# A scan and a gated MLP fused over blocks of tokens: the order of the work at each block's turn

## The chip, the core and the metric

The kernel runs on one core of a Trainium2 chip. The metric is the device time of one execution in microseconds, as the median of several runs. A core has five engines that work through programs of their own and meet at semaphores: TensorE (PE, matrix products), VectorE (DVE), ScalarE (ACT, functions by table), GpSimd (POOL) and SyncE (SP, which starts transfers here). Every engine takes its instructions strictly in the order of its program.

## What is computed

The program is a stack of eight layers on 4096 tokens of 256 numbers, each with a norm before and a norm behind it, and a residual sum. The change touches the fifth and the sixth, a state-space scan (attention's place in layer 2) and a gated MLP:

```python
x = x + _layernorm(_L2_attn_ref(_layernorm(x), ...))
x = x + _layernorm(_L2_ffn_ref(_layernorm(x), ...))

def _L2_attn_ref(x, ...):                     # 512 channels, 16 states
    xc, z = split(x @ in_proj)
    xs = silu(causal_conv4(xc) + conv_b)
    dt, Bm, Cm = split(xs @ x_proj)           # 64, 16, 16
    dt = softplus(dt @ dt_proj + dt_proj_b)
    h = exp(dt * A) * h + dt * Bm * xs        # a scan over time, for each channel and state
    y = sum_states(h * Cm) + D * xs
    return (y * silu(z)) @ out_proj

def _L2_ffn_ref(x, ...):                      # 1024 hidden
    h = silu(w1(x) * s) * (w2(x) * s)
    h = gelu(h1(h) * s)
    h = gelu(h2(h) * s)
    return w3(h) * s
```

## The kernel before

`scan_and_mlp` (line 2099) does both layers in one pass. The tokens are cut into NB = 8 blocks of 512. A loop of nine **steps** n = 0 to 8 runs in every engine: step n does the scan of block n, the scan layer's output product, norms and MLP of block b = n - 1, and the last product and norm of the MLP of block b2 = n - 2. What begins a step, between the last scan of one block and the first of the next, is called the **turn** below.

**Units.** The scan of a block is 64 units k = 0 to 63: 16 states by 4 groups of 128 channels, two groups in the first half (k below 32) and two in the second. Unit k is one exponential on ACT (`exponential`, line 2490, into one of two PSUM banks, so it may run at most two units ahead of the scans), one product on POOL (`unit_product`, 2293, into one of DR = 4 buffers), one scan on DVE (`scan`, 2648, needs both), one product with C on DVE (`times_c`, 2659) and one sum on POOL (`unit_sum`, 2300). The MLP's and the norms' instructions on ACT, DVE, POOL and SP are hung on unit numbers: `if k == 1: post.scalar(...)` puts the scale of a norm behind exponential 1.

**The step size.** Before the first unit, `dt` has to be made: the product `dt` on PE (2375), Abs, Exp and Ln on ACT (2518, 2523, 2527), `dt_linear`, `one_plus` and `step_size` on DVE (2620, 2626 to 2631, 2637 to 2639). Abs writes into `ea`, which is the array `ys` of the block before, so it waits until DVE has gated that block's output (`gated`, 2588 and 2591, counted by `y_ready`).

**PSUM.** All PE results outside the scan go through LB = 4 banks in the fixed order of the list `groups`: a product may start when the result four places before it has been read out (`bank_for`, `taken`). Gate and up of the MLP's first layer are groups of two matmuls each; the hidden layers' groups `hid` of eight; `out` is the MLP's last product, `y` the scan layer's output product, `z` and `in` the two input projections, `xp` the projection x_dbl, `turn` and `turn_l` transposes.

**The MLP on ACT.** `silu_gate` (SiLU on a gate, into one of two buffers) ran in units 9 to 16, one a unit, and DVE's `up_times_gate` (2665) in 8 to 15, one a unit. `GELUS` names the units behind which ACT does two GELUs each. The functions belong to different tables: where Exp and SiLU or GELU follow each other, a load of the table (ACT_TABLE_LOAD) stands between.

**The norms** are made in four parts: statistics on DVE (108, 111), the reciprocal root on POOL (1135 to 1140), the scale on ACT (1145), and for `post` the residual sum on POOL (2304). `post` is behind the scan layer, `pre_l` ahead of the MLP, `post_l` behind it, `pre` ahead of the next scan.

**Transfers.** SP loads the MLP's weights into a ring of WR = 4 buffers of 512 KB (`weights_to`), and the rows of B and C (`bc_load`); the loop of units sets the order of both.

## Time and profile before

| | us |
|---|---|
| median of 3 runs | 5377.04 |
| lowest and highest run | 5374.46 and 5400.65 |
| the profiled execution | 5403.7 |
| its span, first to last instruction | 5401.9 |
| instructions in it | 77,523 |
| PE, DVE, ACT, POOL busy | 4553.4, 3586.3, 2659.0, 2315.1 |

The trace gives every instruction of one execution with its start and its length, and for an engine that stood idle the instruction whose end released it. The fused stage runs from 1940 us to about 3880 us of the span. Step 3 lies in the trace from 2605 us to 2828 us, and stands for steps 2 to 6, whose DVE instructions follow the same pattern.

### The profile page before, as it was taken

How to read it: one execution, taken by the hardware profiler on the slowest of the kernel's cores; microseconds unless marked ns; L12 is line 12 of the kernel's file. 1: busy time of each engine (PE TensorE's matmuls, PEld its weight loads, DVE VectorE, ACT ScalarE, POOL GpSimd, SP SyncE). 2: the span in 40 equal slices, each digit the busy share in tenths (PEclk: the TensorE clock that was granted, in tenths of full speed). 3: DMA queues.
4: the chain of work that ended last, by engine and by line, in shares of the span. 5: the costliest groups of instructions: out<-in, count | busy, mean ns of one | idle time of the engine just before them, and what ended most of it. 6: DMA issues, size and time to landing. Idle time of an engine off the chain costs nothing. (4 is left out here: it accounts for less than half of the span.)

```text
span 5401.9 us, 77523 instructions
## 1 busy us (share of the span) xinstructions
PE 4553.4 (84%) x23572; PEld 2292.7 (42%) x23572; DVE 3586.3 (66%) x5800; ACT 2659.0 (49%) x4933; POOL 2315.1 (43%) x2615
## 2 busy tenths in 40 slices
PE   8799999777978821889888898898879999999598
PEld 4233333443447510344444444444434444444365
DVE  7788887466744468787787877883156666667521
ACT  3466667101323232655656556563137767767221
POOL 4122222323733548768677686784002222222311
PEclk9899999788987965889999899999989999999899
DMA  4111111013223433445354453452131111111000
GB/s 121 54 33 33 33 33 28 6 39 84 55 84 94 110 94 81 122 112 150 107 147 119 116 148 112 139 136 94 56 115 45 45 43 44 53 43 33 18 1 31
DMA packets 261917, 406.64 MB, mean 75 GB/s; under 512 B 53154, under 2 KB 140731, under 8 KB 261307
## 3 DMA queue, kind: packets, MB, share of 16 engines
q1 hardware_dynamic: 254687, 383.81, 25.1%
q0 software_dynamic: 6912, 18.88, 1.4%
q8 instruction: 164, 2.69, 0.2%
q14 instruction: 154, 1.26, 0.1%
HBM read 349.26 MB, written 52.54 MB: 74 GB/s over the span
## 5 line engine op out<-in xcount | busy, mean ns | idle before, releaser
L893 DVE CUSTOM_DVE_ANT_0 banks<-banks,l3s_table 128x1024 f32<-128x1024 f32 x512 | 629.1, 1229 | 307.6 <-PE banks L815 299.9
L999 ACT ACTIVATE l3s_probs<-banks,l3s_far_now 128x512 f32<-128x512 f32 (+4 forms) x1280 | 599.1, 513 | 299.0 <-PE banks L831 154.9
L2293 POOL TENSOR_TENSOR l_dbx<-l_u,l_bc 128x512 f32<-128x512 f32 x512 | 670.7, 1314 | 166.1 <-DVE l_u L2639 164.1
L888 DVE TENSOR_REDUCE l0s_peak<-banks 128x1 f32<-128x1024 f32 x512 | 609.5, 1212 | 141.5 <-PE banks L815 140.7
L2300 POOL TENSOR_TENSOR l_ys<-l_ys,l_hc 128x512 f32<-128x512 f32 x480 | 615.8, 1283 | 183.1 <-DVE l_hc L2659 180.4
L999 ACT ACTIVATE l0s_probs<-banks 128x512 f32<-128x512 f32 x1024 | 535.2, 601 | 275.6 <-PE banks L831 275.3
L2490 ACT ACTIVATE banks<-l_dt,l_decay 128x512 f32<-128x512 f32 x512 | 347.3, 688 | 444.8 <-DVE banks L2648 441.4
L2420 PE MATMUL banks<-l_hb,l_ring 128*128 128x512 f32 x1024 | 455.5, 608 | 19.9 <-issue 19.8
L2420 PE MATMUL banks<-l_ha,l_ring 128*128 128x512 f32 x1024 | 444.2, 594 | 20.2 <-ACT l_hb L2471 10.2
L2648 DVE TENSOR_TENSOR_SCAN banks<-banks,l_carry,l_dbx 128x512 f32<-128x512 f32 x256 | 329.6, 1289 | 137.2 <-ACT banks L2490 96.7
L2648 DVE TENSOR_TENSOR_SCAN banks<-banks,l_dbx 128x512 f32<-128x512 f32 x256 | 314.2, 1229 | 131.3 <-ACT banks L2490 75.1
L831 PE MATMUL banks<-l3s_q_st,l3s_k_st 98*128 98x512 bf16 x1024 | 363.2, 386 | 26.9 <-issue 16.7
L815 PE MATMUL banks<-l3s_k_st,l3s_q_st 96*128 96x512 bf16 x1024 | 318.6, 394 | 48.0 <-PEq L473 27.3
L815 PE MATMUL banks<-l0s_k_st,l0s_q_st 96*128 96x512 bf16 x1024 | 314.6, 389 | 46.5 <-PEq L473 27.0
L2659 DVE TENSOR_TENSOR l_hc<-banks,l_bc 128x512 f32<-128x512 f32 x480 | 325.6, 679 | 0.7 <-POOL l_ys L2300 0.7
L2420 PEld LDWEIGHTS banks<-l_hb,l_ring 128*128 128x128 f32 x1024 | 199.0, 195 | 276.0 <-issue 275.1
L831 PE MATMUL banks<-l0s_q_st,l0s_k_st 98*128 98x512 bf16 x1024 | 309.7, 381 | 5.8 <-ACT l0s_probs L999 2.0
L2420 PEld LDWEIGHTS banks<-l_ha,l_ring 128*128 128x128 f32 x1024 | 193.1, 190 | 267.5 <-issue 254.5
L837 PE MATMUL banks<-l3s_band_parts,identb 128*128 128x220 bf16 (+2 forms) x1920 | 297.2, 263 | 0.0
L848 PE MATMUL banks<-l0s_probs,l0s_vs 128*32 128x256 f32 x4096 | 273.5, 385 | 12.9 <-issue 10.2
L848 PE MATMUL banks<-l3s_probs,l3s_vs 128*32 128x256 f32 x4096 | 277.8, 389 | 1.2 <-ACT l3s_probs L999 0.9
L2407 PE MATMUL banks<-l_xtl,l_ring 128*128 128x512 f32 x512 | 242.0, 626 | 9.8 <-issue 5.7
(446 smaller groups left out, 7830.5 us busy)
## 6 DMA issues: line engine op xcount, KB each, us to landing
l_bc<-l_bc_rows SPq DMA_DIRECT2D x256, 512.0 KB, 5.4
l_ring<-in_l2f_stream SPq DMA_DIRECT2D x176, 512.0 KB, 7.1
l3s_table<-bias_tables SPq DMA_DIRECT2D x16, 960.0 KB, 4.4
y_rows<-l1f_out_b SPq DMA_DIRECT2D x80, 128.0 KB
qk_parts<-l0q_q_parts SPq DMA_DIRECT2D x48, 128.0 KB
qk_parts<-l0q_k_parts SPq DMA_DIRECT2D x48, 128.0 KB
l0s_q_st<-qk_parts SPq DMA_DIRECT2D x64, 96.0 KB
l0s_k_st<-qk_parts SPq DMA_DIRECT2D x64, 96.0 KB
```

The lines of the kernel that those rows point to most:

```text
L815: last = nc.tensor.matmul(s1[t % 2][:, half * 512:(half + 1) * 512], q_st[b % BATCH][0:STACK, t * P:(t + 1) * P], moving(k_st[b % BATCH], ...
L831: last = nc.tensor.matmul(scores, k_st[b % BATCH][0:STACK + 2, t * P:(t + 1) * P], moving(q_st[b % BATCH], STACK + 2, half), start=True, s ...
L848: last = nc.tensor.matmul(outT[q * 32:(q + 1) * 32, :], vs[b % 2][:, kt, :], probs[b % 2][:, kt, q * QUARTER:(q + 1) * QUARTER], start=(kt ...
L888: nc.vector.tensor_reduce(out=peak[:, b % 2, t:t + 1], in_=s1[t % 2], axis=AX, op=ALU.max, negate=True).then_inc(s1_used, 1)
L893: nc.vector.tensor_tensor_reduce(out=s1[t % 2], in0=s1[t % 2], in1=rows, scale=1.0, scalar=LOW, op0=ALU.add, op1=ALU.max, accum_out=peak[: ...
L999: last = nc.scalar.activation(columns(probs[b % 2][:, t, :], c0, c1), scores[:, c0 - half * 512:c1 - half * 512], ACT.Exp, scale=scale, **add)
L2293: nc.gpsimd.tensor_tensor(dbx[:, k % DR], u[:, mt], bc[:, load % BR, 0], ALU.mult).then_inc(dbx_ready, 1)
L2300: nc.gpsimd.tensor_tensor(ys[:, mt], ys[:, mt], hc[:, k % CR], ALU.add).then_inc(add_done, 1)
L2420: last = nc.tensor.matmul(banks[:, bank, :], w[:, c * P:(c + 1) * P], src[:, c, :], start=(c == 0), stop=(c == HT - 1))
L2490: nc.scalar.activation(banks[:, DA + m2, :], dt[:, mt], ACT.Exp, scale=decay[:, mt, st:st + 1])\
L2648: nc.vector.tensor_tensor_scan(out=banks[:, H + m2, :], data0=banks[:, DA + m2, :], data1=dbx[:, k % DR], initial=start, op0=ALU.mult, op1 ...
L2659: nc.vector.tensor_tensor(hc[:, k % CR] if st else ys[:, mt], banks[:, H + m2, :], bc[:, load % BR, 1], ALU.mult).then_inc(hc_ready, 1)
```

## The change

The order of the instructions, and nothing else, is changed. (1) At the turn PE does the output product `y` of the block that has just been scanned first, then the `dt` products, then the MLP's `out` of the block before it; ACT empties `y` ahead of its Abs instructions. (2) The statistics, roots, scales and the residual of `post`, and of `pre_l`, go from units 1 to 5 into the turn (on ACT the scale of `pre_l` goes to unit 1), and with them the SiLUs of z to unit 1 and the reading of `turn_l` to unit 5; the second half of `step_size` goes from unit 1 to unit 5. (3) `GATES` lets ACT do two SiLUs behind each of the units 9, 12, 15, 18, and DVE one `up_times_gate` in that unit and one in the next. (4) The GELUs, the reading of the next block's projections and its SiLUs go to later units.

```diff
--- before.py
+++ after.py
@@ -2112,3 +2112,4 @@
     ADDS = UNITS - CT
-    GELUS = {22: 0, 28: 2, 33: 4, 39: 6, 45: 8, 50: 10, 56: 12, 61: 14}
+    GELUS = {24: 0, 30: 2, 35: 4, 41: 6, 49: 8, 54: 10, 59: 12, 63: 14}
+    GATES = {9: 0, 12: 2, 15: 4, 18: 6}
     LOADS = UNITS // 2
@@ -2167,5 +2168,5 @@
             groups += [f"xp{n}"] if n < NB else []
-            groups += [f"out{b2}.0"] if b2 >= 0 else []
-            groups += [f"dt{n}.{i}" for i in range(CT) if n < NB]
             groups += [f"y{b}.{i}" for i in range(2) if b >= 0]
+            groups += [f"dt{n}.{i}" for i in range(CT) if n < NB]
+            groups += [f"out{b2}.0"] if b2 >= 0 else []
             groups += [f"z{n}.{i}" for i in range(CT) if n < NB]
@@ -2276,4 +2277,4 @@
                         weights_to(first + k // 2)
-                    if n and k in (11, 13, 15, 17):
-                        weights_to(first + 5 + (k - 11) // 2)
+                    if n and k in (11, 13, 16, 19):
+                        weights_to(first + 5 + (11, 13, 16, 19).index(k))
                     if n and k in GELUS:
@@ -2311,2 +2312,6 @@
                 b, b2 = n - 1, n - 2
+                if b >= 0:
+                    post.gpsimd(g, b)
+                    residual(b)
+                    pre_l.gpsimd(g, b)
                 for k in range(UNITS):
@@ -2316,8 +2321,2 @@
                             unit_sum(n, k - DR)
-                    if k == 1 and b >= 0:
-                        post.gpsimd(g, b)
-                    if k == 3 and b >= 0:
-                        residual(b)
-                    if k == 5 and b >= 0:
-                        pre_l.gpsimd(g, b)
                     if k == 8 and b2 >= 0:
@@ -2432,7 +2431,2 @@
                     project_dbl(n)
-                if b2 >= 0:
-                    mlp_out(b2, 0)
-                if n < NB:
-                    for i in range(CT):
-                        project_dt(n, i)
                 if b >= 0:
@@ -2442,2 +2436,7 @@
                     for i in range(CT):
+                        project_dt(n, i)
+                if b2 >= 0:
+                    mlp_out(b2, 0)
+                if n < NB:
+                    for i in range(CT):
                         project_z(n, i)
@@ -2513,2 +2512,5 @@
                 b, b2, more = n - 1, n - 2, n + 1 < NB
+                if b >= 0:
+                    for i in range(2):
+                        take(f"y{b}.{i}", rows[:, 2 * i:2 * i + 2, :].rearrange("p k d -> p (k d)"))
                 if n < NB:
@@ -2519,2 +2521,5 @@
                             .then_inc(abs_done, 1)
+                if b >= 0:
+                    post.scalar(act, b, lambda t: rows[:, t, :], lambda t: rows[:, t, :]).then_inc(post_ready, 1)
+                if n < NB:
                     for i in range(2):
@@ -2527,5 +2532,2 @@
                         nc.scalar.activation(dt[:, half], eb[:, half], ACT.Ln).then_inc(ln_ready, 1)
-                if b >= 0:
-                    for i in range(2):
-                        take(f"y{b}.{i}", rows[:, 2 * i:2 * i + 2, :].rearrange("p k d -> p (k d)"))
                 for k in range(UNITS):
@@ -2534,4 +2536,5 @@
                     if k == 1 and b >= 0:
-                        post.scalar(act, b, lambda t: rows[:, t, :], lambda t: rows[:, t, :]).then_inc(post_ready, 1)
-                    if k == 3 and n < NB:
+                        pre_l.scalar(act, b, lambda t: tokens(b)[:, t, :], lambda t: rows_l[:, t, :])\
+                            .then_inc(rows_l_ready, 1)
+                    if k == 1 and n < NB:
                         wait(act, y_ready, 2 * n)
@@ -2540,5 +2543,2 @@
                     if k == 5 and b >= 0:
-                        pre_l.scalar(act, b, lambda t: tokens(b)[:, t, :], lambda t: rows_l[:, t, :])\
-                            .then_inc(rows_l_ready, 1)
-                    if k == 7 and b >= 0:
                         for c in range(KC):
@@ -2548,4 +2548,5 @@
                             .then_inc(post_l_ready, 1)
-                    if 9 <= k < 9 + HT and b >= 0:
-                        silu_gate(b, k - 9)
+                    if k in GATES and b >= 0:
+                        silu_gate(b, GATES[k])
+                        silu_gate(b, GATES[k] + 1)
                     if k == 21 and more:
@@ -2557,9 +2558,9 @@
                         gelu(b, GELUS[k] + 1)
-                    if k == 33 and more:
+                    if k == 36 and more:
                         for c in range(KC):
                             take_turned(n + 1, c)
-                    if k in (40, 42) and more:
-                        take_x(n + 1, k - 40)
-                        take_x(n + 1, k - 39)
-                    if k == 58 and more:
+                    if k in (43, 44) and more:
+                        take_x(n + 1, 2 * (k - 43))
+                        take_x(n + 1, 2 * (k - 43) + 1)
+                    if k == 59 and more:
                         for i in range(CT):
@@ -2674,4 +2675,5 @@
                     gated(b, 1)
-                if b2 >= 0:
-                    scale_out(b2, 0)
+                    for i in range(2):
+                        moved(v, f"y{b}.{i}")
+                    post.statistics(v, lambda k: rows[:, k, :])
                 if n < NB:
@@ -2680,8 +2682,10 @@
                     one_plus(n, 0)
+                if b >= 0:
+                    v.wait_ge(added, n)
+                    pre_l.statistics(v, lambda t: tokens(b)[:, t, :])
+                if n < NB:
                     one_plus(n, 1)
                     step_size(n, 0)
-                if b >= 0:
-                    for i in range(2):
-                        moved(v, f"y{b}.{i}")
-                    post.statistics(v, lambda k: rows[:, k, :])
+                if b2 >= 0:
+                    scale_out(b2, 0)
                 if n < NB:
@@ -2694,7 +2698,4 @@
                         times_c(n, k)
-                    if k == 1 and n < NB:
+                    if k == 5 and n < NB:
                         step_size(n, 1)
-                    if k == 3 and b >= 0:
-                        v.wait_ge(added, n)
-                        pre_l.statistics(v, lambda t: tokens(b)[:, t, :])
                     if k == 6 and b2 >= 0:
@@ -2703,4 +2704,5 @@
                         post_l.statistics(v, lambda t: scaled[:, t, :])
-                    if 8 <= k < 8 + HT and b >= 0:
-                        up_times_gate(b, k - 8)
+                    for j in (0, 1):
+                        if k - j in GATES and b >= 0:
+                            up_times_gate(b, GATES[k - j] + j)
                     if k == 18 and more:
```

ACT_TABLE_LOAD stands 280 times in ACT's program before, and 217 times now. The three places below are those on which the times rest. Names are those of the arrays; `l` in front stands for the stage.

On ACT, step 2's turn, from the reading of x_dbl to the SiLUs of z, before (`l_ys` takes Abs and Exp, `l_dt` Ln, `l_rows` the reading of `y` and the scale of `post`):

```order
L2471 ACTIVATE l_x_dbl<-banks 96x512
L2518 ACTIVATE l_ys<-banks,l_dt_b 128x512 x4
L2523 ACTIVATE l_ys<-l_ys 128x1024 x2
L2527 ACT_TABLE_LOAD
L2527 ACTIVATE l_dt<-l_hc 128x1024 x2
L2471 ACTIVATE l_rows<-banks 128x512 x2
L2490 ACT_TABLE_LOAD
L2490 ACTIVATE banks<-l_dt,l_decay 128x512 x2
L1145 ACTIVATE l_rows<-l_rows,l_post_shift,l_post_rstd 128x256 x4
L2490 ACTIVATE banks<-l_dt,l_decay 128x512 x2
L2471 ACT_TABLE_LOAD
L2471 ACTIVATE l_zs<-banks 128x512 x4
```

and now:

```order
L2470 ACTIVATE l_ha<-banks,l_sc 128x512 x2
L2470 ACTIVATE l_x_dbl<-banks 96x512
L2470 ACTIVATE l_rows<-banks 128x512 x2
L2520 ACTIVATE l_ys<-banks,l_dt_b 128x512 x4
L1145 ACTIVATE l_rows<-l_rows,l_post_shift,l_post_rstd 128x256 x4
L2528 ACT_TABLE_LOAD
L2528 ACTIVATE l_ys<-l_ys 128x1024 x2
L2532 ACT_TABLE_LOAD
L2532 ACTIVATE l_dt<-l_hc 128x1024 x2
L2489 ACT_TABLE_LOAD
L2489 ACTIVATE banks<-l_dt,l_decay 128x512 x2
L1145 ACTIVATE l_hb<-x,l_pre_l_shift,l_pre_l_rstd 128x256 x4
```

The reading of `y` and the scale of `post` now stand ahead of the Exp, the last two GELUs behind the last exponential, and a table load ahead of the Exp on `l_ys`.

On PE, the same turn, before:

```order
L2368 MATMUL banks<-l_xs,l_w_x 96x512 x4
L2396 MATMUL banks<-l_ring,l_ha 128x256 x16
L2375 MATMUL banks<-l_x_dbl,l_w_dt 128x512 x4
L2384 MATMUL banks<-l_w_out,l_xs 128x256 x16
L2360 MATMUL banks<-l_xt,l_w_in 128x512 x8
L2396 MATMUL banks<-l_ring,l_ha 128x256 x16
L2341 MATMUL banks<-ident,l_hb 128x128 x8
```

and now:

```order
L2367 MATMUL banks<-l_xs,l_w_x 96x512 x4
L2383 MATMUL banks<-l_w_out,l_xs 128x256 x16
L2374 MATMUL banks<-l_x_dbl,l_w_dt 128x512 x4
L2395 MATMUL banks<-l_ring,l_ha 128x256 x16
L2359 MATMUL banks<-l_xt,l_w_in 128x512 x8
L2395 MATMUL banks<-l_ring,l_ha 128x256 x16
L2340 MATMUL banks<-ident,l_hb 128x128 x8
```

`y` (array `l_w_out`) stands behind the projection x_dbl (array `l_w_x`) at once; `dt` and `out` (array `l_ring` with `l_ha`) stand behind it.

On DVE, the same turn from behind the end of gating, before (`l_hb<-banks,l_so` is the scaling of `out`):

```order
L2614 TENSOR_TENSOR l_hb<-banks,l_so 128x256 x2
L2620 TENSOR_SCALAR l_u<-banks,l_dt_b 128x512 x4
L2626 TENSOR_SCALAR l_hc<-l_ys 128x1024
L2628 SCALAR_TENSOR_TENSOR l_ys<-l_hc,l_ys 128x1024
L2631 TENSOR_TENSOR l_ys<-l_u,l_ys 128x1024
L2626 TENSOR_SCALAR l_hc<-l_ys 128x1024
L2628 SCALAR_TENSOR_TENSOR l_ys<-l_hc,l_ys 128x1024
L2631 TENSOR_TENSOR l_ys<-l_u,l_ys 128x1024
L2637 TENSOR_TENSOR l_dt<-l_dt,l_ys 128x1024
L2639 TENSOR_TENSOR l_u<-l_dt,l_xs 128x1024
L108 BN_STATS l_post_stats<-l_rows 128x6 x4
L111 BN_AGGR l_post_mean_var<-l_post_stats 128x2 x4
```

and now:

```order
L2621 TENSOR_SCALAR l_u<-banks,l_dt_b 128x512 x4
L2627 TENSOR_SCALAR l_hc<-l_ys 128x1024
L2629 SCALAR_TENSOR_TENSOR l_ys<-l_hc,l_ys 128x1024
L2632 TENSOR_TENSOR l_ys<-l_u,l_ys 128x1024
L108 BN_STATS l_pre_l_stats<-x 128x6 x4
L111 BN_AGGR l_pre_l_mean_var<-l_pre_l_stats 128x2 x4
L2627 TENSOR_SCALAR l_hc<-l_ys 128x1024
L2629 SCALAR_TENSOR_TENSOR l_ys<-l_hc,l_ys 128x1024
L2632 TENSOR_TENSOR l_ys<-l_u,l_ys 128x1024
L2638 TENSOR_TENSOR l_dt<-l_dt,l_ys 128x1024
L2640 TENSOR_TENSOR l_u<-l_dt,l_xs 128x1024
L2615 TENSOR_TENSOR l_hb<-banks,l_so 128x256 x2
```

The statistics of `post` (the same two rows, right behind gating and ahead of this piece now) and those of `pre_l` stand ahead of and inside the chain that makes the step size, and the scaling of `out` behind it.

## Rows read from the trace of the kernel before

**Rows 1.** Windows: busy us of PE, PEld, DVE, ACT, POOL; PE clock; DMA share; GB/s

```profile
2626.00:2850.00 224.00, 197.24 (x480) 95.34 (x480) 180.86 (x210) 133.00 (x171) 167.97 (x144) 0.93 0.46 127
```

**Rows 2.** Timeline of DVE at step 3's turn: start, length, engine, line, operands, idle before

```profile
2604.81 1.23 DVE L2591 TENSOR_TENSOR l_xs<-l_xs,l_zs 128x1024 f32<-128x1024 f32 x1
...
2611.38 1.23 DVE L2628 SCALAR_TENSOR_TENSOR l_ys<-l_hc,l_ys 128x1024 f32<-128x1024 f32 x1
...
2618.53 1.23 DVE L2639 TENSOR_TENSOR l_u<-l_dt,l_xs 128x1024 f32<-128x1024 f32 x1
2619.67 1.40 DVE L108 BATCH_NORM_STATS2 l_post_stats<-l_rows 128x6 f32<-128x256 f32 x4
...
2621.45 2.43 DVE L2648 TENSOR_TENSOR_SCAN banks<-banks,l_carry,l_dbx 128x512 f32<-128x512 f32 x2
```

**Rows 3.** Timeline of PE at the same turn

```profile
2598.77 2.84 PE L2375 MATMUL banks<-l_x_dbl,l_w_dt 64*128 64x512 f32 x6
...
2608.82 8.41 PE L2384 MATMUL banks<-l_w_out,l_xs 128*128 128x256 f32 x32
```

**Rows 4.** Timeline of ACT and of POOL at the same turn

```profile
2609.51 1.99 ACT L2523 ACTIVATE l_ys<-l_ys 128x1024 f32<-128x1024 f32 x2
...
2624.26 2.07 ACT L1145 ACTIVATE l_rows<-l_rows,l_post_shift,l_post_rstd 128x256 f32<-128x256 f32 x4 [3.78 <-POOL l_post_shift L1140]
...
2622.29 0.20 POOL L1135 TENSOR_TENSOR l_post_rstd<-l_post_mean_var,eps 128x4 f32<-128x4 f32 x1
...
2624.03 0.20 POOL L1140 TENSOR_TENSOR l_post_shift<-l_post_shift,l_post_rstd 128x4 f32<-128x4 f32 x1
```

**Rows 5.** Timeline of PE and of ACT where step 8 begins, after an idle PE

```profile
3697.61 10.13 PE L2384 MATMUL banks<-l_w_out,l_xs 128*128 128x256 f32 x32 [7.92 <-DVE l_xs L2591]
...
3704.32 0.60 ACT L2471 ACTIVATE l_rows<-banks 128x512 f32<-128x512 f32 x1 [18.20 <-PE banks L2384]
```

**Rows 6.** Timeline of DVE: scans of units 10, 20, 37, 38, 46, 57, 63

```profile
2656.09 1.28 DVE L2648 TENSOR_TENSOR_SCAN banks<-banks,l_carry,l_dbx 128x512 f32<-128x512 f32 x1
...
2665.54 0.75 DVE L2665 SCALAR_TENSOR_TENSOR l_ha<-banks,l_sc,l_hb 128x512 f32<-128x512 f32 x1
2667.55 1.29 DVE L2648 TENSOR_TENSOR_SCAN banks<-banks,l_carry,l_dbx 128x512 f32<-128x512 f32 x1 [1.25 <-ACT banks L2490]
...
2691.13 1.26 DVE L2648 TENSOR_TENSOR_SCAN banks<-banks,l_carry,l_dbx 128x512 f32<-128x512 f32 x1
...
2733.32 1.29 DVE L2648 TENSOR_TENSOR_SCAN banks<-banks,l_carry,l_dbx 128x512 f32<-128x512 f32 x1
...
2743.45 1.28 DVE L2648 TENSOR_TENSOR_SCAN banks<-banks,l_carry,l_dbx 128x512 f32<-128x512 f32 x1
...
2765.85 1.29 DVE L2648 TENSOR_TENSOR_SCAN banks<-banks,l_carry,l_dbx 128x512 f32<-128x512 f32 x1 [6.48 <-ACT banks L2490]
...
2808.76 1.29 DVE L2648 TENSOR_TENSOR_SCAN banks<-banks,l_carry,l_dbx 128x512 f32<-128x512 f32 x1
...
2821.47 1.29 DVE L2648 TENSOR_TENSOR_SCAN banks<-banks,l_carry,l_dbx 128x512 f32<-128x512 f32 x1
```

**Rows 7.** Timeline of ACT and PE in the gates' units, of POOL behind them

```profile
2663.53 1.28 ACT L2471 ACT_TABLE_LOAD   x1
...
2665.61 3.67 PE L2407 MATMUL banks<-l_xtl,l_ring 128*128 128x512 f32 x8 [0.34 <-issue]
...
2706.56 14.00 PE L2420 MATMUL banks<-l_ha,l_ring 128*128 128x512 f32 x32 [1.24 <-DMA l_ring<-in_l2f_stream]
...
2707.88 1.26 POOL L2293 TENSOR_TENSOR l_dbx<-l_u,l_bc 128x512 f32<-128x512 f32 x1
...
2710.34 1.27 POOL L2293 TENSOR_TENSOR l_dbx<-l_u,l_bc 128x512 f32<-128x512 f32 x1
```

**Rows 8.** Timeline of ACT at unit 45's GELUs and at unit 58

```profile
2763.12 0.69 ACT L2471 ACTIVATE l_ha<-banks,l_sc 128x512 f32<-128x512 f32 x1 [5.57 <-PE banks L2420]
...
2805.77 1.67 ACT L2484 ACTIVATE l_xs<-l_xs 128x512 f32<-128x512 f32 x3
```

8 lines of the change are left out of this document (4 added, 4 removed).

## The prediction

> **What bounds the kernel now.** I read in this order: the busy time by stretch, the timelines of all engines across one turn, then the scans of one block on DVE, each with what ended the idle time before it. In a full step no engine is busy all the time: of 224 us PE works 197, DVE 181, POOL 168, ACT 133 [rows 1]. So the length of a step is not the work of one engine but a chain that changes hands, and the reader should follow the scans, since every block needs all 64 of them and they are on the chain at each place. Step 3 is taken for steps 2 to 6. The gating of the old block begins at 2604.81 and the first new scan at 2621.45, 16.6 us of turn [rows 2]. The later scans give the stretches of the block [rows 2, 6]: unit 0 to 10 takes 34.6 us, 10 to 20 35.0, 20 to 37 42.2, 37 to 38 (the other gating) 10.1, 38 to 46 22.4, 46 to 57 (the four convolutions) 42.9, 57 to 63 12.7. Undisturbed, DVE needs 2.0 us for a unit's scan and product (2665.54 to 2667.55 is one gate product and a wait of 1.25 us that ACT ended, so a gate unit takes 4.0) [rows 6]. POOL needs 2.46 us for a unit (2707.88 to 2710.34) [rows 7]. From 10 to 20 ACT bounds, from 20 to 37 POOL; at unit 46 DVE waits 6.48 us, because ACT sits in front of a GELU for 5.57 us, which PE had not reached [rows 6, 8].
>
> **The turn.** The zero of the times in this part is 2606.0, the end of gating (2604.81 + 1.23), and the first scan stands at 15.4 [rows 2]. Three of the four `dt` products were then already done, at 2598.77, in the shadow of the last scans [rows 3]. That is what the new order takes away: `y` needs the gated block, so it can't start before 0, and everything behind it on PE, `dt` too, waits for it. The cost of `y` is 8.41 us if PE comes from work [rows 3] and 10.13 behind an idle stretch of 7.92, with the first half only there 6.7 us after the start [rows 5]. PE will have been idle for over 10 us here (it has nothing left but x_dbl), so I take 10.1 and keep 8.4 for the range. Then:
> - four `dt` at 0.95 (2.84 / 3) to 13.9, the last Abs (0.7) to 14.6 (Abs as a GELU) [rows 3, 8];
> - beside it ACT reads `y` (0.60, to 10.8), DVE does the statistics (1.40, and 0.4 for the four small ones behind, from 2619.67 to 2621.45) to 12.6, POOL the roots (2622.29 to 2624.23, 1.9) to 14.5 [rows 2, 4, 5];
> - ACT scales `post` (2.07) to 16.7, loads the table for Exp (1.28, new here: the last thing on ACT is now a GELU) to 18.0, first Exp (1.0) to 19.0 [rows 4, 7];
> - DVE: `one_plus` (0.7 + 1.25 + 1.25 = 3.2, its middle instruction) to 22.2 [rows 2], statistics of `pre_l` (1.8) to 24.0 (the residual is there by then), second `one_plus` 3.2 to 27.2, `step_size` (2 x 1.25) to 29.7;
> - POOL's first product (1.26) to 31.0; with the scaling of `out` and hand-overs the first scan is at 31.4 instead of 15.4 [rows 2, 7].
>
> The turn gets **16 us longer**.
>
> **Unit 0 to 10, 4.7 us shorter.** Ten units at 2.0, the half `step_size` of 2.5 (4.5 before, when POOL's residual ran beside it, so 2.5 to 4.5), `out`'s scaling and statistics 2.5, together 25. Waits: the scale of `pre_l`, the SiLUs of z and two loads (2.1 + 2.4 + 2.6) hold exponential 2 back so that DVE waits 3.3; reading `turn_l` costs 0.9, since `out`'s second half, which waits for z's banks, puts the transposes at about unit 5; the root of `post_l` on POOL holds its product 9 back, 1.5. With 0.8 less for the first scan pair: 29.9.
>
> **Unit 10 to 20, 2.4 us shorter.** Loads fall from 16 to 8 a step here, so ACT would need only 3 x 0.69 + 2 x 0.69 + 2 x 1.28 = 6.0 us for three units [rows 7, 8]. But the four banks now bind: up j + 2 may be computed when DVE has read up j, and gate j + 3 stands behind it. One cycle of three units is: scan 1.29, product 0.67, `up_times_gate` 0.75, two PE groups 3.67, SiLU 0.69, load 1.28, exponential 0.69 = 9.1 us, against 7.4 for POOL's three units and 12.0 for three before [rows 6, 7, 8]. The gates stretched over twelve units instead of eight, so the gain is small: 9.6 for 10 to 13 (POOL adds the residual `residual_l` of 2.3 here, which the slow gate units hid before), 18.4, and 4.6 for the last unit with the statistics of `pre`: 32.6.
>
> **Unit 20 to 57.** POOL keeps its pace of 2.46, so 20 to 37 stays 42.2; PE gets to the hidden layers some 20 us later than before: the first needs the last gate product, which stands 31.4 + 29.9 + 32.6 + 2.8 = 97 us behind gating instead of 15.4 + 34.6 + 6.5 x 4.0 = 76, and two GELUs wait for it, 0.8 in all. 38 to 46 loses its wait: the GELUs are at unit 49 now, and PE, still some 16 us late, is through before; 22.4 becomes 16.7, **5.7 less**. 46 to 57 is DVE's own work and stays.
>
> **Unit 57 to 63, 3.8 us longer.** The block's SiLUs used to start on ACT at 2805.77, in the shadow of the last convolution (DVE's next scan is at 2808.76) [rows 6, 8]. Now they follow two GELUs behind exponential 59: 1.28 + 1.37 + 1.28 + 2.5 + 1.28 + 0.69 = 8.4 us until the next exponential, of which DVE has 3.9 in hand; it waits 4.5. The wait of 0.8 at unit 61's GELUs goes.
>
> **SP and the rest.** The weights' loads go later with the GELUs, each still behind the product that frees its buffer, at least 7 us ahead of its user; one such wait is 1.24 now [rows 7], taken as unchanged. Loads of B and C don't move.
>
> **Sum.** A full step: 16.0 - 4.7 - 2.4 + 0.8 - 5.7 + 3.8 = +7.8, five times = 39. Step 1 has no `out` and no `post_l`, its table load is not new, and its gains in the gates are larger: +3. Step 7 has no next block, so neither the gain of 5.7 nor the loss of 3.8: +9. Step 0: +1. In step 8 `y` leads anyway and its `out` fills idle PE time: 0. Together +52: the profiled execution would go from 5403.7 to 5456. It lies 26.7 above the median of 5377.04, so I carry the difference over: **5429**.
>
> **A rule of the skill.** A table load takes 1.28 us in the trace, and the exponential follows at once (2663.53 + 1.28) [rows 7]. The program has 280 loads, 63 more than now; taken whole that is 81 us. The Trainium skill ("ScalarE: Activation LUTs", Table sets: the hidden batching unit) says to batch calls by set, which is what the pairs of gates do, and gives about 2.66 us for a switch with its drain; by that figure it would be 168 us, an estimate, and the sum would be a gain. The trace doesn't bear out the drain, and has ACT busy 133 of 224 us, so the rule counts only where ACT bounds.
>
> **Rivals.**
> 1. *The loads' whole time comes back.* If ACT set the pace of the whole step, 63 x 1.28 = 81 us and the six waits of about 6.2 us (37) come off, against seven turns (112) and six late SiLUs (23): +17; and as the late SiLUs wait for loads that the 81 has counted already, -6: 5371. For it speaks 12 us a step of ACT-bound gate units, against it POOL's 2.46 right behind them. If the turn were shorter too (`y` at 8.4, `post`'s scale and the load beside `dt`: 5 us), it would reach 5371 - 35 = 5336, the one way to a clearly faster kernel.
> 2. *The gates run at POOL's pace.* If PE's two groups are ready before ACT asks, 10 to 20 is 24.6 + 2.3 + 1.9 = 28.8, 3.8 less a step; PE is then early enough for the GELUs as well (0.8): 7.8 - 4.6 = 3.2, in all about +22: 5399, not slower by what can be told. It decides at a cycle of 8 us or less.
> 3. *PE becomes late.* The hidden layers start 20 us later, and two GELUs wait already. If the clock after the longer idle stretch makes y and z slower by 5 us, these waits grow one for one: +4 to 5 a step, +30: 5459 and more.
>
> **How the numbers follow.** Forecast (5405 to 5450) 0.55; rival 3 (5450 to 5485) 0.15; rival 2 and milder mixes (5385 to 5405) 0.13; rival 1 at 5371 0.10, at 5336 0.07. A measurement tells about 0.5% (27 us) from no change. Slower by more: 0.70 (0.55 + 0.15); within: 0.23 (0.13 + 0.10); faster: 0.07. The range goes from 5372 to 5475.
>
> **What would show it.** In the profile after: PE idle for over 10 us before L2383's first product, and that product ahead of dt; the first scan 31 us behind the end of gating; gate units with 9 us for three; no wait of 6 us for the GELUs in the convolutions' units; one wait of 4 to 5 us behind exponential 59. It would be wrong if the exponentials of `dt` didn't wait for `post`'s scale, or if steps came out at 224 us or less.

## The result and the profile after

| | before | after |
|---|---|---|
| median, measured side by side | 5386.72 us | 5468.94 us |
| lowest and highest run | 5374.46 and 5400.65 | 5456.45 and 5481.87 |
| the profiled execution, its span | 5403.7, 5401.9 | 5481.87, 5480.1 |
| ACT busy | 2659.0 | 2580.8 |

The changed kernel takes 1.0152 times as long (95% interval 1.0108 to 1.0196): 82 us more, where 52 were forecast. The time lies inside the range of 5372 to 5475, and the sign is the one forecast. But it lies 40 us above the forecast of 5429 and outside the band around it (5405 to 5450), in the band that rival 3 had been given with a chance of 0.15. 10 of these us are the kernel before, whose median is 5386.72 here where the forecast started from 5377.04; the other 30 have no term in the sum.

The change did what it says on ACT, 78 us less work there. None of it shows in the time. The chain of a step, read off the starts of DVE's scans as in [rows 2, 6], shows why. Each number is the mean of steps 2 to 6; the third column is what the prediction added.

| stretch | before | after | measured | predicted |
|---|---|---|---|---|
| turn (scan 63 to the next scan 0) | 23.0 | 39.0 | +16.0 | +16.0 |
| unit 0 to 10 | 34.6 | 29.7 | -4.9 | -4.7 |
| unit 10 to 20 | 35.0 | 34.9 | -0.1 | -2.4 |
| unit 20 to 38 | 52.3 | 52.4 | +0.1 | +0.8 |
| unit 38 to 46 | 23.1 | 16.7 | -6.4 | -5.7 |
| unit 46 to 57 | 42.9 | 46.6 | +3.7 | 0 |
| unit 57 to 63 | 12.7 | 16.2 | +3.5 | +3.8 |
| a step | 223.7 | 235.4 | +11.7 | +7.8 |

Five full steps cost 58.6 us more, step 1 14.9 (218.0 to 233.0), step 7 12.7 (195.0 to 207.7), step 0 0.3: 86.5 for steps 0 to 7. Everything else took 8.3 less in this execution, 7.0 of it ahead of the first scan (1982.8 to 1975.8), in layers that the change doesn't touch, so the span grew by 78.2.

**The turn.** The timeline of PE at step 3's turn, after (start, length, engine, line, operands, idle before; answers to [rows 3]):

```profile
2625.41 10.14 PE L2383 MATMUL banks<-l_w_out,l_xs 128*128 128x256 f32 x32 [5.97 <-DVE l_xs L2592]
2635.47 3.70 PE L2374 MATMUL banks<-l_x_dbl,l_w_dt 64*128 64x512 f32 x8
2639.10 7.17 PE L2395 MATMUL banks<-l_ring,l_ha 128*128 128x256 f32 x32
```

ACT in the same turn (answers to [rows 4]), and DVE (answers to [rows 2]):

```profile
2632.13 0.60 ACT L2470 ACTIVATE l_rows<-banks 128x512 f32<-128x512 f32 x1 [12.06 <-PE banks L2383]
...
2640.19 2.07 ACT L1145 ACTIVATE l_rows<-l_rows,l_post_shift,l_post_rstd 128x256 f32<-128x256 f32 x4 [0.29 <-POOL l_post_shift L1140]
2642.28 1.28 ACT L2528 ACT_TABLE_LOAD   x1
2643.57 2.01 ACT L2528 ACTIVATE l_ys<-l_ys 128x1024 f32<-128x1024 f32 x2
```

```profile
2624.13 1.23 DVE L2592 TENSOR_TENSOR l_xs<-l_xs,l_zs 128x1024 f32<-128x1024 f32 x1
2636.28 1.41 DVE L108 BATCH_NORM_STATS2 l_post_stats<-l_rows 128x6 f32<-128x256 f32 x4 [10.93 <-ACT l_rows L2470]
...
2644.66 0.69 DVE L2627 TENSOR_SCALAR l_hc<-l_ys 128x1024 f32<-128x1024 f32 x1 [3.64 <-ACT l_ys L2528]
...
2657.05 2.49 DVE L2649 TENSOR_TENSOR_SCAN banks<-banks,l_carry,l_dbx 128x512 f32<-128x512 f32 x2 [0.82 <-POOL l_dbx L2294]
```

The four `dt` products, of which three used to be done 4.4 us before gating ended, now end 13.8 us behind its end (2625.36). Exp waits for `post`'s scale and a table load, and the first scan stands 31.7 us behind gating. PE had been idle for only 5.97 us when `y` began, where the prediction expected over 10: it was late with the hidden layers and the projection x_dbl.

**The gates.** Windows of the three rounds of gates in step 3: us, busy us of PE, PEld, DVE, ACT, POOL (instructions), granted clock of PE, DMA share, GB/s.

```profile
2678.00:2687.50 9.50, 9.40 (x16) 3.84 (x16) 6.20 (x13) 4.94 (x7) 7.21 (x9) 0.76 0.43 150
2689.30:2698.20 8.90, 8.83 (x16) 3.53 (x16) 4.94 (x6) 5.86 (x8) 8.90 (x7) 0.81 0.82 174
2700.10:2707.30 7.20, 7.13 (x16) 2.96 (x16) 4.84 (x6) 4.80 (x6) 7.20 (x7) 1.00 0.35 76
```

The same 16 matmuls take 9.40, 8.83 and 7.13 us. A granted clock of 1.00 is the 2.4 GHz level; 0.76 and 0.81 mean that part of the stretch ran at 1.2 GHz. PE had stood idle for 6.79 us before the first round, 1.91 before the second and 1.97 before the third. Before the change it had pauses of 0.3 to 0.4 us in these units, and the clock stood at 1.00. Which rounds are slow differs from step to step: in steps 2 and 4 it is the first and the third, and a fourth round, of 12 matmuls, takes 7.1 us at 0.76 in steps 1 to 4, for what takes 5.4 at 1.00 (units_only below).

**The convolution.** DVE and POOL at the first convolution of step 3, after:

```profile
2793.92 0.67 DVE L2660 TENSOR_TENSOR l_hc<-banks,l_bc 128x512 f32<-128x512 f32 x1
2794.51 6.26 DVE L2599 TENSOR_SCALAR l_xs<-l_xc,l_taps,l_conv_b 128x512 f32<-128x512 f32 x1
2800.85 2.40 DVE L2602 SCALAR_TENSOR_TENSOR l_xs<-l_xc,l_taps,l_xs 128x512 f32<-128x512 f32 x3
```

```profile
2794.31 1.30 POOL L2294 TENSOR_TENSOR l_dbx<-l_u,l_bc 128x512 f32<-128x512 f32 x1
...
2799.20 1.30 POOL L2294 TENSOR_TENSOR l_dbx<-l_u,l_bc 128x512 f32<-128x512 f32 x1
2805.12 1.27 POOL L2301 TENSOR_TENSOR l_ys<-l_ys,l_hc 128x512 f32<-128x512 f32 x1 [4.63 <-DVE l_hc L2660]
```

The same instruction before took 0.93 us, and the three behind it 4.09:

```profile
2769.64 0.93 DVE L2598 TENSOR_SCALAR l_xs<-l_xc,l_taps,l_conv_b 128x512 f32<-128x512 f32 x1
2770.65 4.09 DVE L2601 SCALAR_TENSOR_TENSOR l_xs<-l_xc,l_taps,l_xs 128x512 f32<-128x512 f32 x3
```

POOL works through five instructions 1.22 us apart until 2800.5, and DVE's ends at 2800.8. Over the program this line grew from 43.6 to 75.8 us, 32.2 = 6 x 5.4: once a step, in steps 1 to 6. Step 0 had the long one before the change too (46 to 57 took 47.1 there).

**The last units.** DVE behind exponential 59, and PE's waits for weights:

```profile
2847.55 1.29 DVE L2649 TENSOR_TENSOR_SCAN banks<-banks,l_carry,l_dbx 128x512 f32<-128x512 f32 x1 [4.31 <-ACT banks L2489]
```

```profile
2813.23 14.00 PE L2419 MATMUL banks<-l_hb,l_ring 128*128 128x512 f32 x32 [1.65 <-DMA l_ring<-in_l2f_stream]
2835.29 16.15 PE L2419 MATMUL banks<-l_hb,l_ring 128*128 128x512 f32 x32 [8.06 <-DMA l_ring<-in_l2f_stream]
```

The first is the wait of 4.5 us that was forecast. The others are not: over the program PE waits 57.0 us for weights in the second hidden layer, where before it waited for none; the 8.0 us that it waited for them in the first hidden layer before are gone (the row of the page; busy us, mean ns | idle before, what ended it):

```profile
L2419 PE MATMUL banks<-l_hb,l_ring 128*128 128x512 f32 x1024 | 456.5, 607 | 57.2 <-DMA l_ring<-in_l2f_stream 57.0
```

### The profile page after: what moved, and what is told of

Its sections match the earlier page's. It is cut to its first block and busy times, and to the rows that moved or that the text cites. A ratio compares the mean times of both kernels' runs of the same rounds, so it can differ in the third digit from the quotient of the medians.

```text
span 5480.1 us, 77460 instructions
## 1 busy us (share of the span) xinstructions
PE 4565.1 (83%) x23572; PEld 2298.9 (42%) x23572; DVE 3583.6 (65%) x5800; ACT 2580.8 (47%) x4870; POOL 2327.1 (42%) x2615
## 5 line engine op out<-in xcount | busy, mean ns | idle before, releaser
L2294 POOL TENSOR_TENSOR l_dbx<-l_u,l_bc 128x512 f32<-128x512 f32 x512 | 658.5, 1291 | 69.3 <-DVE l_u L2640 57.2
L2406 PE MATMUL banks<-l_xtl,l_ring 128*128 128x512 f32 x512 | 272.0, 691 | 94.5 <-DVE l_ha L2666 41.1
L848 PE MATMUL banks<-l0s_probs,l0s_vs 128*32 128x256 f32 x4096 | 273.5, 385 | 12.8 <-issue 10.2
```

The source lines that it names most:

```text
L848: last = nc.tensor.matmul(outT[q * 32:(q + 1) * 32, :], vs[b % 2][:, kt, :], probs[b % 2][:, kt, q * QUARTER:(q + 1) * QUARTER], start=(kt ...
L2294: nc.gpsimd.tensor_tensor(dbx[:, k % DR], u[:, mt], bc[:, load % BR, 0], ALU.mult).then_inc(dbx_ready, 1)
```

## The experiments

Every kernel was timed beside the kernel before, whose median was between 5386 and 5398 us in these groups; ratios are to that. The table gives the same stretches for all (means of steps 2 to 6).

| kernel | ratio, 95% interval | turn | 0-10 | 10-20 | 20-38 | 38-46 | 46-57 | 57-63 | step |
|---|---|---|---|---|---|---|---|---|---|
| before | 1 | 23.0 | 34.6 | 35.0 | 52.3 | 23.1 | 42.9 | 12.7 | 223.7 |
| after | 1.0152 (1.0108, 1.0196) | 39.0 | 29.7 | 34.9 | 52.4 | 16.7 | 46.6 | 16.2 | 235.4 |
| turn_only | 1.0103 (1.0065, 1.0141) | 38.0 | 28.7 | 35.0 | 52.3 | 22.4 | 42.9 | 12.7 | 232.0 |
| units_only | 1.0028 (1.0010, 1.0046) | 26.2 | 34.6 | 34.5 | 52.4 | 16.7 | 46.6 | 16.2 | 227.2 |
| gates_only | 1.0033 (1.0011, 1.0054) | 23.0 | 34.6 | 35.0 | 55.3 | 21.0 | 42.9 | 12.7 | 224.4 |
| gelus_only | 1.0033 (1.0013, 1.0054) | 26.6 | 34.6 | 35.0 | 52.4 | 16.7 | 46.5 | 16.2 | 228.0 |
| y_first_norms_old | 1.0152 (1.0120, 1.0184) | 35.8 | 34.0 | 34.6 | 52.4 | 16.7 | 46.6 | 16.2 | 236.2 |
| gelus_last_back | 1.0155 (1.0128, 1.0183) | 37.6 | 29.1 | 34.0 | 52.4 | 16.7 | 46.6 | 19.1 | 235.5 |
| bank_early | 1.0103 (1.0074, 1.0131) | 38.4 | 28.4 | 35.2 | 52.4 | 16.7 | 46.6 | 16.2 | 233.9 |
| conv_stt | 1.0156 (1.0124, 1.0187) | 38.4 | 29.4 | 34.9 | 52.4 | 16.7 | 47.6 | 16.2 | 235.5 |
| last_back_loads_old | 1.0080 (1.0049, 1.0110) | 38.4 | 29.5 | 34.9 | 52.4 | 16.7 | 44.9 | 12.7 | 229.3 |
| gelu49_loads_old | 0.9942 (0.9918, 0.9966) | 23.0 | 34.6 | 35.0 | 52.3 | 16.0 | 44.1 | 12.7 | 217.8 |
| gelu49_pool_wait | 0.9915 (0.9892, 0.9939) | 23.0 | 34.6 | 35.0 | 52.3 | 16.0 | 42.6 | 12.7 | 216.2 |
| gelu49_pool_waits4 | 0.9866 (0.9843, 0.9889) | 24.1 | 34.6 | 35.0 | 52.3 | 16.0 | 38.5 | 12.7 | 213.2 |

### The change in parts

**turn_only**: the kernel after, with gates, GELUs and the loads and projections that go with them as before; only the turn is changed, items (1) and (2).

```diff
-    GELUS = {24: 0, 30: 2, 35: 4, 41: 6, 49: 8, 54: 10, 59: 12, 63: 14}
-    GATES = {9: 0, 12: 2, 15: 4, 18: 6}
+    GELUS = {22: 0, 28: 2, 33: 4, 39: 6, 45: 8, 50: 10, 56: 12, 61: 14}
...
-                    if k in GATES and b >= 0:
-                        silu_gate(b, GATES[k])
-                        silu_gate(b, GATES[k] + 1)
+                    if 9 <= k < 9 + HT and b >= 0:
+                        silu_gate(b, k - 9)
...
```

> The kernel before with the turn's new order alone: y first, both norms' steps moved up, the second step_size and the SiLUs of z moved; gates one a unit and GELUs, projections and SiLUs at the old units. Theory (the turn is the loss): the turn goes from 22.8 to 39 us in each of steps 2 to 6, units 0 to 10 from 34.6 to about 30, units 10 to 20 stay at 35 or more, the wait for the GELUs before unit 46 stays (22 to 24 us for units 38 to 46), so a step is 11 to 14 us longer and the kernel 75 to 100 us slower than before. Rival (the later units are the loss): the PE and ACT work keeps its old places, the gain at units 0 to 10 pays most of the turn, under 30 us slower.

Measured: ratio 1.0103, some 55 us, less than the 75 to 100 of my theory and more than the 30 of the rival. The turn alone grows by 15.0 us a step and units 0 to 10 give 5.9 back. So the turn is the largest part, 8.3 of the 11.7 us a step.

**units_only**: the kernel before with the new places of gates and GELUs and the old turn, items (3) and (4).

```diff
-    GELUS = {22: 0, 28: 2, 33: 4, 39: 6, 45: 8, 50: 10, 56: 12, 61: 14}
+    GELUS = {24: 0, 30: 2, 35: 4, 41: 6, 49: 8, 54: 10, 59: 12, 63: 14}
+    GATES = {9: 0, 12: 2, 15: 4, 18: 6}
...
```

> The kernel before with the later units alone: gates two at a time, GELUs, projections and SiLUs later; the turn as before. Theory (the turn is the loss): turn 22.8 and units 0 to 10 at 34.6 as before; units 10 to 20 between 30 and 35, units 38 to 46 down from 22.4 to 16.7, units 46 to 57 up from 42.9 to 46.6 (a slow first convolution), units 57 to 63 up from 12.7 to 16.2 (the block's SiLUs behind two GELUs), in all 0 to 5 us less a step, the kernel 0 to 35 us faster. Rival (the later units are the loss): 50 us slower or more.

Measured: 1.0028, a little slower where a gain was expected. 46 to 57 and 57 to 63 took what was expected; the turn didn't, it became 3.2 us longer though nothing in it had been moved.

The steps of this kernel also price the clock in the gates. Their instructions are the same, but the granted clock is not, and units 10 to 20 follow it. Windows of the last three rounds, in step 2 and in step 5 (us, busy us of PE (instructions), granted clock, DMA share, GB/s):

```profile
2442.59:2449.73 7.14, 7.13 (x16) 1.00 0.83 184
2452.26:2459.40 7.14, 7.13 (x16) 1.00 0.28 90
2461.37:2466.80 5.43, 5.43 (x13) 1.00 0.61 187
```

```profile
3122.08:3130.92 8.84, 8.83 (x16) 0.81 0.77 182
3132.89:3141.73 8.84, 8.83 (x16) 0.81 0.21 59
3143.69:3150.81 7.12, 7.12 (x13) 0.76 0.63 194
```

With all three at 1.00 the stretch takes 32.1 us (the prediction had 32.6), with one slow 33.8 (step 3), with two 34.9 (steps 4 and 6), with three 36.7.

**gates_only** and **gelus_only** split units_only once more: the line `GATES` with its users alone, and the line `GELUS` with the reading of projections and the SiLUs alone.

> The kernel before with the gates two at a time alone (SiLUs behind units 9, 12, 15, 18, products in the unit and the next, the weights' loads with them). Theory (the four banks bind the pairs): a cycle of three units takes 9 us at full clock, up to 11 us where the clock granted to PE is lower, so units 10 to 20 take 30 to 36 us against 35.0, and as PE starts the hidden layers later, the wait of 6 us for the GELUs at unit 46 grows and GELUs at units 22, 28 and 33 wait as well: 5 to 15 us more a step, the kernel 30 to 90 us slower. Rival (the table loads are the cost): 56 loads of 1.28 us come off the gates, units 10 to 20 fall to 29, the kernel 20 to 40 us faster.

Measured: 1.0033, 18 us where at least 30 were expected. In steps 2 to 6 units 10 to 20 stay at 35.0, although 8 table loads a step are gone; 20 to 38 is 3.0 longer, since PE then reaches the hidden layers later and ACT waits in front of early GELUs (3.73 us at 2703.19 in step 3). 38 to 46, which was expected to grow, is 2.1 shorter. The gates in pairs buy nothing on the chain.

> The kernel before with the later units for GELUs, projections and the block's SiLUs alone. Theory: units 38 to 46 fall from 22.4 to 16.7; the first convolution's first instruction takes about 6 us instead of 0.9, since POOL is then at work, so units 46 to 57 rise from 42.9 to 46.6; units 57 to 63 rise from 12.7 to about 16; in all 0 to +1 us a step, the kernel within 10 us of before. Rival (the convolution's length has another cause than POOL's work beside it): units 46 to 57 stay at 42.9 and the kernel is 20 us faster.

Measured: 1.0033, and 4.3 us a step where at most 1 was expected. The wait ahead of unit 46 is gone (-6.4), and 3.6, 3.5 and 3.6 come back in 46 to 57, in 57 to 63 and in the turn. The turn is seen on PE, just ahead of step 3 of gelus_only:

```profile
2575.84 3.60 PE L2368 MATMUL banks<-l_xs,l_w_x 128*96 128x512 f32 x8
2579.28 7.07 PE L2396 MATMUL banks<-l_ring,l_ha 128*128 128x256 f32 x32
2586.28 3.70 PE L2375 MATMUL banks<-l_x_dbl,l_w_dt 64*128 64x512 f32 x8
```

`out` (L2396) can't begin before the last GELU, which now stands at unit 63, and in the old order the `dt` products are behind it on PE: they start at 2586.28, behind the end of gating (2585.82), where three of them used to be done ahead of it [rows 3]. On ACT a table load is put ahead of Exp as well. In the kernel after `dt` is behind `y` anyway, and the turn grows by 16.0 us, not by 15.0 + 3.2: the two delays share 2.2. Over a whole step turn_only and units_only still add up (8.3 + 3.5 = 11.8 against 11.7), since the kernel after gives less back in the units than those two together (1.0 of it in units 0 to 10). It is gates_only and gelus_only that together cost more than units_only (0.7 + 4.3 against 3.5): the early GELUs for which gates_only waits stand later in units_only.

### Which half of the turn

**y_first_norms_old**: the kernel after, norms back in units 1 to 5, on DVE, ACT and POOL.

```diff
-                if b >= 0:
-                    post.gpsimd(g, b)
-                    residual(b)
-                    pre_l.gpsimd(g, b)
                 for k in range(UNITS):
...
+                    if k == 1 and b >= 0:
+                        post.gpsimd(g, b)
+                    if k == 3 and b >= 0:
+                        residual(b)
+                    if k == 5 and b >= 0:
+                        pre_l.gpsimd(g, b)
```

> The kernel after, with y's product still ahead of dt and out on PE, but with the norms' steps back where they were (scaling of post at unit 1, residual at 3, statistics and scaling of pre_l at 3 and 5, SiLUs of z at 3). It asks which half of the turn's edit lengthens it. My theory is that y's product ahead of dt is the larger part. From rows of the kernel with the turn's edit alone (end of gating 2598.70, y's product 9.18 us, first scan 2629.34, so 30.6 against 15.4 before): without post's scaling on ACT (2.07) and the statistics of pre_l between the two halves (1.8) and the 1.4 and 0.4 of post's statistics ahead of dt_linear, about 5 us of the 15.2 go, so the turn should be 33 to 35 us from the last scan of a block to the first of the next (39.0 in the kernel after, 22.8 before), while units 0 to 10 go back from 29.7 to 34.6. Per step nothing is gained: between 2 us shorter and 3 longer, the whole within 20 us of the kernel after, 5450 to 5490. The rival says that the norms' steps are what lengthens the turn, since PE has the whole time of the norms to catch up: then the turn is 27 us or less and the whole under 5430.

Measured: turn 35.8, units 0 to 10 34.0, ratio 1.0152 as the kernel after. So what is left of the change costs 12.8 of the turn's 16.0 us. 3.2 of it units_only has as well, from the late GELUs and their table load; `y` ahead of `dt` adds the other 9.6. The norms' steps only move between the turn and the units: 3.2 us on one side, 4.3 on the other. The rival (27 us) is out.

### The bank of `out` and the gates

**bank_early**

```diff
-                    if k == 6 and b2 >= 0:
+                    if k == 4 and b2 >= 0:
                         scale_out(b2, 1)
+                    if k == 6 and b2 >= 0:
                         v.drain()
```

> The kernel after, with one move: DVE scales the second half of out at unit 4 instead of unit 6 (its statistics stay at 6), which frees a bank that PE needs for the second gate. In the kernel after PE waits 6.79 us for that instruction and starts again at 2678.03, though out had been done at 2668.1. Unit 4 is worked at 2671, so PE starts 5 to 6 us earlier, and the second SiLU of a gate, which came at 2684.04 behind a wait of 4.52 us, is ready when ACT asks. My theory (the missing 2.4 us of units 10 to 20 and more went into this wait) gives 4.5 us less from unit 10 to 20: 30.4 instead of 34.9 in steps 2 to 6, nothing in step 1, in all 20 to 27 us less than the kernel after. The rival says that the gates' own round of PE, ACT and DVE at 10.8 us for three units sets the pace from the first pair on, so that an earlier start only moves a wait: then 10 to 20 stays above 33.5 and the whole within 8 us of the kernel after.

Measured: 10 to 20 at 35.2, so my theory falls for this stretch. The first pair of SiLUs does come without a wait, but then PE stands idle until `up_times_gate` frees a bank, and the next round is slow again:

```profile
2692.57 8.72 PE L2406 MATMUL banks<-l_xtl,l_ring 128*128 128x512 f32 x16 [5.36 <-DVE l_ha L2666]
```

The wait only moved. Against the kernel after the ratio is lower (1.0103 to 1.0152, with intervals that overlap), and steps 1 to 7 take 10 us less in the profiled executions, so something is gained, but in units 0 to 10 (1.3 a step) and the turn (0.6), not where I had looked for it. The turn's share is the clock over `y` again: `y` takes 8.67 us at 0.82 in step 3 and 10.02 at 0.71 in step 4, and the turn 37.6 and 39.0. With the windows above that leaves the rounds' own length. In the kernel after it is 10.8 us from one round's second SiLU to the next (2684.04 to 2694.84) where the 16 matmuls between take 8.83, and 9.1 (to 2703.95) where they take 7.13.

### The convolution

**conv_stt**

```diff
-                nc.vector.tensor_scalar(mine, xc[:, c, 0:TB], taps[:, c, 0:1], conv_b[:, c:c + 1], ALU.mult, ALU.add)
+                nc.vector.scalar_tensor_tensor(out=mine, in0=xc[:, c, 0:TB], scalar=taps[:, c, 0:1],
+                                               in1=conv_b[:, c:c + 1].to_broadcast([P, TB]), op0=ALU.mult, op1=ALU.add)
```

> The kernel after, with the first of the four steps of each convolution written as another instruction of DVE: a SCALAR_TENSOR_TENSOR that adds the bias as a broadcast operand, in place of the TENSOR_SCALAR; the values are the same. In the kernel after the first TENSOR_SCALAR (2794.51) takes 6.26 us against 0.93 before, and ends as POOL, which had run without a gap, falls idle; the SCALAR_TENSOR_TENSORs take 0.8 to 1.4 beside a busy POOL. My theory is that this form alone is held up while POOL has work without a gap. Then the stretch of units 46 to 57 falls from 46.6 to 42 to 44, 3 to 4 us a step in seven steps, and the whole is 18 to 28 us under the kernel after. The rival says that any large instruction of DVE would be held there, since what matters is that POOL has four units in hand: then the new first step takes 5 us or more too, the stretch stays at 46 or above and the time doesn't change.

Measured: the other instruction takes 6.51 us in the same place, and the stretch is 47.6. The form is not the cause; the rival holds.

```profile
2797.75 6.51 DVE L2599 SCALAR_TENSOR_TENSOR l_xs<-l_xc,l_taps,l_conv_b 128x512 f32<-128x512 f32 x1
2804.34 2.40 DVE L2603 SCALAR_TENSOR_TENSOR l_xs<-l_xc,l_taps,l_xs 128x512 f32<-128x512 f32 x3
```

### The last GELUs, and the loads behind them

**gelus_last_back**

```diff
-    GELUS = {24: 0, 30: 2, 35: 4, 41: 6, 49: 8, 54: 10, 59: 12, 63: 14}
+    GELUS = {24: 0, 30: 2, 35: 4, 41: 6, 49: 8, 54: 10, 56: 12, 61: 14}
...
-                    if k == 59 and more:
+                    if k == 58 and more:
```

> The kernel after, with only its last two pairs of GELUs back at units 56 and 61 and the block's SiLUs back at 58. My theory is that the SiLUs behind two GELUs and the exponential of unit 59 cost the 4.31 us that DVE waits at 2847.55, and that GELUs at unit 63 leave the table of GELU on ACT, so that the exponential of dt pays a load (1.28 at 2642.28) in the turn. So the stretch of units 57 to 63 falls from 16.1 to 12.7 and the turn from 39.0 to 37.7: 4.7 us a step, 33 us for six to seven steps, and the whole comes to 5427 to 5445. The rival says that with an earlier GELU PE, which runs late behind the longer turn, isn't there yet, and DVE waits at units 56 and 61 instead: then 46 to 57 grows by what 57 to 63 loses, and the whole stays within 10 us of the kernel after.

Measured: 1.0155, no gain. The turn did get 1.4 us shorter and the wait behind exponential 59 went, but 57 to 63 took 19.1. ACT, then DVE, at unit 61:

```profile
2871.56 0.69 ACT L2470 ACTIVATE l_ha<-banks,l_sc 128x512 f32<-128x512 f32 x1 [6.18 <-PE banks L2419]
```

```profile
2874.28 1.29 DVE L2649 TENSOR_TENSOR_SCAN banks<-banks,l_carry,l_dbx 128x512 f32<-128x512 f32 x1 [7.51 <-ACT banks L2489]
```

PE was late, and not from the longer turn. It had waited 8.29 us for weights:

```profile
2855.02 16.50 PE L2419 MATMUL banks<-l_hb,l_ring 128*128 128x512 f32 x32 [8.29 <-DMA l_ring<-in_l2f_stream]
```

SP issues the loads at the units of `GELUS`, so a later unit number also moved the loads; this pair was issued at unit 54 (2847.62).

**last_back_loads_old**: the same with a table of their own for SP's loads.

```diff
+    LOADS_AT = {22: 0, 28: 2, 33: 4, 39: 6, 45: 8, 50: 10, 56: 12, 61: 14}
...
-                    if n and k in GELUS:
-                        weights_to(first + 10 + GELUS[k])
+                    if n and k in LOADS_AT:
+                        weights_to(first + 10 + LOADS_AT[k])
```

> The kernel after, with its last two pairs of GELUs back at units 56 and 61 and the block's SiLUs at 58 (as in gelus_last_back, which gained nothing), and now also with SP's loads of the hidden layers' weights back at the units of the kernel before (22, 28, 33, 39, 45, 50, 56, 61). In gelus_last_back units 57 to 63 took 19.3 us, since PE had waited 8.29 us for weights (2855.02) whose load SP had issued at unit 54 (2847.62). My theory, formed from that run, is that the loads' place, and not the length of the turn, makes PE late at unit 61. Then PE has no such wait, units 57 to 63 take 12.7 to 13.5, the turn stays at 37.6, and the whole is 35 to 45 us under gelus_last_back, 5440 to 5452 beside 5398 of the kernel before. The rival says that PE is late from the longer turn itself (its hidden layers start 20 us later): then it still isn't there at unit 61, 57 to 63 stays at 17 or more, and the gain is under 15 us.

Measured: 1.0080, 57 to 63 at 12.7. The 88 us that gelus_last_back stood over its own before became 43. The gain of 45 us is the upper end of what was expected, because 46 to 57 fell too (46.6 to 44.9), which I had not foreseen.

### Is there a faster kernel

**gelu49_loads_old**: the kernel before, with the one move that had gained and nothing that had cost.

```diff
-    GELUS = {22: 0, 28: 2, 33: 4, 39: 6, 45: 8, 50: 10, 56: 12, 61: 14}
+    GELUS = {22: 0, 28: 2, 33: 4, 39: 6, 49: 8, 52: 10, 56: 12, 61: 14}
+    LOADS_AT = {22: 0, 28: 2, 33: 4, 39: 6, 45: 8, 50: 10, 56: 12, 61: 14}
...
-                    if n and k in GELUS:
-                        weights_to(first + 10 + GELUS[k])
+                    if n and k in LOADS_AT:
+                        weights_to(first + 10 + LOADS_AT[k])
```

> The kernel before, with the GELUs of unit 45 moved to 49 and those of 50 to 52, the last two pairs, the SiLUs and all loads where they are. My theory: units 38 to 46 lose the wait of 6.5 us (22.4 to 23.7 down to 16.7), and about 3.7 us of it come back in units 46 to 57, since POOL, no longer held up behind DVE's wait, works without a gap when the first convolution starts, whose first instruction then takes 6 us instead of 0.93; the last stretch and the turn stay (12.7 and 22.8). So 2 to 3 us a step in six steps, 12 to 18 us, ratio 0.997. The rival says that the slow convolution belongs to the later hidden layers and not to POOL: then 46 to 57 stays at 42.9 and the whole is 35 us faster, ratio 0.993.

Measured: 0.9942, between theory and rival. 38 to 46 lost 7.1, and only 1.2 of it came back. The instruction of 6 us that the theory expected isn't there. The wait ahead of unit 46 is gone and POOL works without a gap, as in the kernel after, yet the first convolution of step 3 begins like this, on DVE and on POOL:

```profile
2741.43 1.01 DVE L2599 TENSOR_SCALAR l_xs<-l_xc,l_taps,l_conv_b 128x512 f32<-128x512 f32 x1
2742.51 4.94 DVE L2602 SCALAR_TENSOR_TENSOR l_xs<-l_xc,l_taps,l_xs 128x512 f32<-128x512 f32 x3
```

```profile
2740.88 1.28 POOL L2301 TENSOR_TENSOR l_ys<-l_ys,l_hc 128x512 f32<-128x512 f32 x1
2742.10 1.46 POOL L2294 TENSOR_TENSOR l_dbx<-l_u,l_bc 128x512 f32<-128x512 f32 x1
```

DVE waits for the one POOL instruction that is under way, and then the two take turns. The convolution costs about 1 us more than before, and not 3.6.

**gelu49_pool_wait**

```diff
                         unit_product(n, k)
+                        if k == 49 and n + 1 < NB:
+                            wait(g, conv_ready, (n + 1) * CT + 1)
```

> gelu49_loads_old with one wait more: behind its product for unit 49 POOL waits until the first convolution of the next block is done, so that it is idle while DVE works on it. My theory is that DVE's first instruction there is held up by POOL's unbroken work. Then it takes 0.7 to 1.4 us instead of 6.3, units 46 to 57 take 41.5 to 43.5 instead of 46.6 in all seven steps that have convolutions (step 0 too, 47.1 so far), POOL's later products come in time but for a wait of DVE of about 1 us, and the whole is 32 to 40 us under the kernel before, ratio 0.993. The rival says that POOL's work has to be done anyway, and that DVE pays at the next units what it saved (POOL needs 2.46 us for a unit, DVE 2.0): then the stretch stays above 45.5 and the ratio at 0.997.

Measured: 0.9915, the stretch at 42.6 in every step, in step 0 too (47.1 before). The long first instruction, which this family still had in step 0, fell from 6.88 to 2.02 us there. In step 3 the whole first convolution went from 6.03 to 4.36 us. POOL's work, held back by a few microseconds, didn't come back as a wait of DVE; 0.3 us came back as longer second and third convolutions. The median against that of gelu49_loads_old, in the same group, is 12.0 us lower; the two intervals overlap, the steps' stretches do not.

**gelu49_pool_waits4**

```diff
-                        if k == 49 and n + 1 < NB:
-                            wait(g, conv_ready, (n + 1) * CT + 1)
+                        if k in (49, 52, 55, 58) and n + 1 < NB:
+                            wait(g, conv_ready, (n + 1) * CT + (k - 46) // 3)
```

> gelu49_pool_wait, with POOL held in the same way for the other three convolutions: behind its products for units 52, 55 and 58 it waits until convolution 2, 3 and 4 of the next block is done. In gelu49_pool_wait the second convolution's three SCALAR_TENSOR_TENSORs take 4.10 us with two POOL instructions beside them (1.44 and 1.72), where the same three took 2.40 with POOL idle. My theory: each convolution lasts as long as POOL's work beside it, so an idle POOL takes up to 1.7 us off each of the last three and up to 2.5 off the first; but POOL starts each stretch 1 to 2 us later, and DVE then waits for its products for part of it. So units 46 to 57 go from 42.6 to 39 to 41 us in seven steps, 11 to 25 us under gelu49_pool_wait, ratio 0.988 to the kernel before. The rival says that POOL's 2.46 us for a unit against DVE's 2.0 between two convolutions leaves nothing to hold back: what DVE saves in a convolution it waits for POOL right behind it, the stretch stays at 42 or above, and the ratio at 0.991.

Measured: 5324.59 us, 0.9866 (0.9843 to 0.9889), the fastest kernel here: 1.3% under before, 2.8% under the kernel after. The fourth convolution of step 3 on DVE, and POOL beside it:

```profile
2755.11 0.84 DVE L2601 TENSOR_SCALAR l_xs<-l_xc,l_taps,l_conv_b 128x512 f32<-128x512 f32 x1
2756.02 3.25 DVE L2604 SCALAR_TENSOR_TENSOR l_xs<-l_xc,l_taps,l_xs 128x512 f32<-128x512 f32 x3
```

```profile
2755.60 1.48 POOL L2294 TENSOR_TENSOR l_dbx<-l_u,l_bc 128x512 f32<-128x512 f32 x1
2759.36 1.27 POOL L2301 TENSOR_TENSOR l_ys<-l_ys,l_hc 128x512 f32<-128x512 f32 x1 [2.28 <-DVE l_xs L2604]
```

With one POOL instruction beside it the three take 3.25 us; with two 4.1, with three 4.94, with none 2.40. POOL is later at the end of the block now, and the turn pays 1.1 us for that.

## Why the prediction was right, and where it was not

**The turn** was right in its mechanism and in its size: 31.7 us from gating to the first scan against 31.4, `y` 10.14 against 10.1, the end of `post`'s scale 16.9 us behind gating against 16.7. y_first_norms_old shows that its largest piece is the one named first, that `dt` loses the shadow of the last scans. The size of `y` was luck in part. The prediction took 10.1 because PE would have been idle for over 10 us; it had been idle for 5.97. In turn_only it was idle for 18.46 us there, and `y` took 9.18 at a granted clock of 0.78. So a longer pause did not mean a slower `y`.

**Unit 0 to 10** (-4.9 against -4.7), **38 to 46** (-6.4 against -5.7) and **57 to 63** (+3.5 against +3.8, the wait 4.31 against 4.5) were right too. PE is late, but at unit 49 that didn't decide.

**Unit 10 to 20** is the first step that failed: 34.9 for 32.6. The round of banks was the right limit, and its length of 9.1 us is what rounds at a clock of 1.00 show. The others take 10.8. The term that was too small is PE's 3.67 us for two groups, taken from rows at 1.00 [rows 7]: with two SiLUs at a time PE stops between rounds, and in most rounds the granted clock is lower. The steps of units_only show that this is what was missing: 32.1 us with three rounds at 1.00, 34.9 with two of them slow. Rival 3 had this clock for `y` and `z`, and not for the gates. In step 1 the same error is larger (+2.5 instead of a gain), where I had counted on larger gains than elsewhere; its turn grew by 15.7 like the others, and its convolution by 3.6. (In conv_stt, whose gates are the same code, step 1 takes 34.6 and not 37.8, with one round at 1.00.) Step 1 at +3, measured +14.9, was the single worst term.

**Unit 46 to 57, "DVE's own work and stays"**, is the second: +3.7 in six steps, 22 us. DVE's instructions stayed, their length didn't. The wait of 6.5 us at unit 46 had let POOL run out of work; with the wait gone POOL has five instructions in hand when the convolution starts, and DVE's instruction waits for them. 5.3 of the 6.4 us that the wait was worth go there, while the three instructions behind it get 1.7 back. The step of the prediction that failed is that it asked who waits for whom by semaphore only. conv_stt rules out the form of the instruction. That DVE waits for POOL is shown by step 0 of gelu49_pool_wait, where holding POOL took the instruction from 6.88 to 2.02 us, and by the ends: in all 54 long ones of these kernels it ends 0.28 us behind the last of POOL's unbroken run (0.55 in the other form). But the wait that is gone isn't the whole of the cause, since gelu49_loads_old has lost it too and has no long instruction in steps 1 to 6.

**The weights** were said to arrive at least 7 us ahead of their user, but for a wait of 1.24. That wait is gone, and PE waits 57.0 us for them in the second hidden layer. The GELUs of the kernel after don't pay for it, as they come late as well; gelus_last_back shows what it costs when they don't. Units 46 to 57 may: they take 46.6 in gelus_last_back and 44.9 in last_back_loads_old, which differ in the loads alone.

**The rivals.** The loads' whole time did not come back: ACT has 78 us less work, and DVE's chain shows none of it. Rival 2 needed a cycle of 8 us or less in the gates; the shortest is 9.1. Of rival 3 the place was wrong and the mechanism partly right. The missing 34.5 us (86.5 in steps 0 to 7 against 52) are 11.9 in step 1, 3.7 in step 7, -0.7 in step 0 and 19.6 in five full steps: a step is 3.9 above the forecast, 2.3 for the gates and 3.7 for the convolution, less 2.1 in the other stretches.

**What stays open.** Why DVE's first instruction sometimes waits for POOL's whole run and sometimes for one instruction. In the seven kernels with late loads and POOL without a gap, steps 1 to 6 have the long form in 41 of 42 cases; in gelu49_loads_old and last_back_loads_old, with the loads at their old units, in 1 of 12; in step 0, which loads no weights, always, unless POOL is held. That accounts for 46.6 against 44.1 and 44.9. But a long and a short one can start at the same point of a POOL instruction, so the traces don't show what decides it, or what the loads have to do with it. For the clock, no run held it and changed only the pauses, and why one round is back at 1.00 behind a pause as long as another's isn't shown.

## What to carry to other kernels

Before a product is put ahead of others on an engine, look at what the others were hidden behind: here three `dt` products lay in the shadow of the last scans, and one that needs the freshest data in front of them took all of that away, on the longest chain of the program. A wait that is removed may have been doing something, so look at which engine it held back, and whether the next instruction takes longer when that engine works beside it. And if one table sets the places of two things (GELUs and the loads of weights), give each its own before you move one.

## What the hardware showed

**DVE and POOL.** The convolution's instructions read SBUF alone. They take 2.40 us for three with POOL idle, 3.25 with one POOL instruction beside them, 4.1 with two and 4.94 with three (POOL's own 1.27 become 1.44 to 1.72). The first of a convolution, 0.54 us with POOL idle, usually ends 0.28 us behind the POOL instruction that was under way. In the kernel after it takes 6.26 us in step 3, through five POOL instructions, until POOL runs dry. An unbroken POOL alone doesn't bring this about: in gelu49_loads_old it takes 0.91 to 1.53 us in steps 1 to 6. The scans and the products with C, which have one operand in PSUM, stay at 1.29 and 0.67 beside the same POOL. The Trainium skill ("SBUF — State Buffer", Who interferes with whom) says that VectorE and GpSimd share one pair of ports, that an instruction of VectorE in a two-port mode, or with two SBUF inputs while GpSimd's reads SBUF, contends for it and others don't, and that the one which starts first holds it for its whole instruction. The trace agrees on who contends. On how long, it agrees for most of these instructions and differs for the long ones: by that rule DVE would wait for the one instruction of POOL that is under way, 1.3 us at most, and there it waited for all five. Holding POOL back with a semaphore during the four convolutions took units 46 to 57 from 44.1 us to 38.5, and 1.1 came back in the turn.

**The clock.** The window of `y` in step 3 of the kernel after (columns as in the gates' windows):

```profile
2625.40:2635.50 10.10, 10.09 (x33) 8.16 (x33) 0.00 (x0) 0.60 (x1) 0.00 (x0) 0.70 0.65 175
```

Behind 5.97 us of idle PE the granted clock over `y` was 0.70, a mean between the 1.2 GHz level (0.5) and the 2.4 GHz level (1.0), and `y` took 10.14 us where it had taken 8.41 [rows 3]. In turn_only it took 9.18 at 0.78 behind 18.46 us of idle PE, and in bank_early 8.67 at 0.82 behind 5.76 and 10.02 at 0.71 behind 6.05: the length of the pause doesn't tell the clock. Behind pauses of 6.79 and 1.91 us rounds of 16 matmuls ran at 0.76 and 0.81, 9.40 and 8.83 us for what takes 7.13 at 1.00, and a pause of 1.97 had 1.00 behind it.
